# Route, scan and routed experts on one core: order of the work between tiles in two of the stages

## The reference

```python
scores = sigmoid(x @ router_w)
scores_grouped = (scores + router_bias).reshape(T, G, E // G)
group_scores = top_k(scores_grouped, 2).sum(-1)       # the best 4 groups stay open
top_k_index = top_k(masked, K)
tkw = scores[top_k_index] / sum * 2.5
gate, up = ragged_dot(xs, w_gate), ragged_dot(xs, w_up)   # rows sorted by expert, 512 columns
down = ragged_dot(silu(gate) * up, w_down)
shared = silu(x @ sw_gate) * (x @ sw_up) @ sw_down
```

## Time and profile before

| | |
|---|---|
| Median of three runs | 11768.19 us |
| Profiled execution | 11704.35 us |
| Its span | 11702.8 us |
| Mean granted TensorE clock | 0.985 |
| TensorE (PE) busy | 11303.2 us (97%) |
| Weight loads (PEld) | 9279.1 us (79%) |
| VectorE busy | 4611.8 us (39%) |
| ScalarE busy | 2989.1 us (26%) |
| GpSimd busy | 4299.9 us (37%) |

### The profile page before, as it was taken

The page is one execution under the profiler, slowest core; times in us unless marked ns, Lnnn a source line. Parts: engine busy times, 40 slices in busy tenths (PEclk is TensorE's granted clock), DMA queues, the critical chain, the costliest instruction groups (busy, mean ns, idle before and its releaser), DMA issues.

```text
span 11702.8 us, 200733 instructions
## 1 busy us (share of the span) xinstructions
PE 11303.2 (97%) x50496; PEld 9279.1 (79%) x50497; DVE 4611.8 (39%) x6239; ACT 2989.1 (26%) x4098; POOL 4299.9 (37%) x4236
## 2 busy tenths in 40 slices
PE   8999689998999999999999999999998999999998
PEld 7888467776888888888888888878887787888887
DVE  5666566664232323333323233232334323223222
ACT  2122244442222222222222222222223223222221
POOL 2555442222333333333333333333333333333333
PEclk9999799999999999999999999999999999999999
DMA  4333366675444444454544454454555545444443
GB/s 160 132 132 133 110 168 178 179 177 148 96 115 100 117 96 118 119 136 99 137 97 119 97 156 98 97 134 96 137 143 158 140 97 155 97 97 117 97 97 85
DMA packets 918208, 1451.51 MB, mean 124 GB/s; under 512 B 314530, under 2 KB 585058, under 8 KB 895048
## 3 DMA queue, kind: packets, MB, share of 16 engines
q0 software_dynamic: 212800, 623.06, 25.2%
q10 hardware_dynamic: 384512, 383.85, 11.8%
q1 hardware_dynamic: 320776, 443.28, 11.5%
HBM read 853.67 MB, written 596.15 MB: 124 GB/s over the span
## 4 chain that ended last, share of the span: by engine, by line
PE 64%; DVE 3%; issue 3%; DMA 3%; ACT 1%; DVEq 1%; ACTq 1%; POOL 0%; SPq 0%; POOLq 0%
PE pd L2002 22%; PE pg L66 7%; PE pg L67 7%; PE pu L66 7%; PE pg L68 7%; PE pu L68 7%; PE pu L67 7%; DMA activated<-av 2%; DVE w_lo L1908 2%; ACT w_hi L1817 1%; DMA aq<-activated 1%; ACTq L1589 1%; DVEq L1589 0%; DVE aT L1931 0%; DVE xT L1920 0%
## 5 line engine op out<-in xcount | busy, mean ns | idle before, releaser
L1772 POOL DMA_INDIRECT xq<-xn_rows,idx_q x2124 | 2191.5, 1032 | 936.6 <-issue 485.2
L1780 POOL DMA_INDIRECT out_rows<-y,idx_s x528 | 865.9, 1640 | 4472.0 <-issue 4462.2
L1956 DVE SCALAR_TENSOR_TENSOR av<-pu,scale,sg 128x512 f32<-128x512 f32 x528 | 396.6, 751 | 3598.3 <-PE pu L68 3537.3
L66 PE MATMUL pg<-w_hi,x_hi 128*128 128x512 f32 x4224 | 1645.5, 390 | 49.5 <-DVE x_lo L1924 39.4
L66 PE MATMUL pu<-w_hi,x_hi 128*128 128x512 f32 x4224 | 1644.2, 389 | 6.0 <-DVEq L1973 6.0
L67 PE MATMUL pg<-w_lo,x_hi 128*128 128x512 f32 x4224 | 1644.5, 389 | 0.0
L68 PE MATMUL pg<-w_hi,x_lo 128*128 128x512 f32 x4224 | 1644.4, 389 | 0.0
L67 PE MATMUL pu<-w_lo,x_hi 128*128 128x512 f32 x4224 | 1643.2, 389 | 0.0
L68 PE MATMUL pu<-w_hi,x_lo 128*128 128x512 f32 x4224 | 1643.2, 389 | 0.0
L1821 ACT ACTIVATE x_hi<-xT 128x1024 fp32r<-128x1024 f32 x530 | 562.8, 1062 | 3885.4 <-DVE xT L1920 3885.4
L2002 PE MATMUL pd<-w_hi,a_hi 128*128 128x512 f32 x4224 | 1143.6, 393 | 91.7 <-ACT a_hi L1837 91.3
(11 more groups left out here) (286 smaller groups left out, 14560.9 us busy)
## 6 DMA issues: line engine op xcount, KB each, us to landing
stage<-in_w_all SPq DMA_DIRECT2D x174, 1024.0 KB, 8.6
activated<-av ACTq DMA_DIRECT2D x528, 256.0 KB
aq<-activated ACTq DMA_DIRECT2D x528, 256.0 KB
rep<-steps ACTq DMA_DIRECT2D x192, 512.0 KB
xq<-xn_rows,idx_q POOLq DMA_INDIRECT x2124
xt<-in_x SPq DMA_DIRECT2D x64, 512.0 KB, 4.6
xn_rows<-xn SPq DMA_DIRECT2D x64, 512.0 KB, 2.6
xn_turned<-sx_hi SPq DMA_DIRECT2D x64, 512.0 KB
```

The lines of the kernel that those rows point to most:

```text
L66: m(dst, hi, whi[:, cols], start=begin, stop=False)
L1772: g.indirect_dma_start(out=xq[q][:, n], out_offset=None, in_=xn_q, in_offset=bass.IndirectOffsetOnAxis(ap=idx_q[q][:, n:n + 1], axis=0))\
L1780: g.indirect_dma_start(out=out, out_offset=bass.IndirectOffsetOnAxis(ap=idx_s[q][:, 0:1], axis=0), in_=y[q][:], in_offset=None, compute_op ...
L1956: v.scalar_tensor_tensor(out=av[:], in0=pu[:], scalar=scale[q][:].bitcast(F32), in1=sg[:], op0=ALU.mult, op1=ALU.mult).then_inc(av_ready, 1)
```

## The change

In the expert stage, three things change. VectorE turns the activations of t-1 ahead of the low parts of the down weights. The rows of t+1 (not t+2) are turned in tile t, and this stands on both engines near the head of the tile: behind `a_lo` on VectorE, behind `a_hi` on ScalarE, and so ahead of the silu and of the gate and up weights of the next expert. The reads of `fresh` and `runs` stand ahead of the waits and are made in every tile; gathers and lists of rows run two tiles ahead instead of three. In the route stage the choice of experts has five parts: old part 1 is cut behind its second search, parts 0 and 1 stand in k = 1, the one-hot part 2 in k = 2, part 3 in k = 3 and part 4 (old 3) in k = 0; turning `z` moves from k = 1 to k = 2 on TensorE, and its eviction from k = 2 to k = 3 on ScalarE.

```diff
@@ route stage, TensorE / ScalarE
-                    if k == 1 and not known(c, 0):
+                    if k == 2 and not known(c, 0):
                         z_turned(c - 1)
-                    if k == 2 and not known(c, 0):
+                    if k == 3 and not known(c, 0):
                         z_row(c - 1, 1 - r)
@@ route stage, VectorE
-                        route(c - 2, r, 3)
-                    if k < 3 and not known(c, 0):
-                        route(c - 1, 1 - r, k)
+                        route(c - 2, r, 4)
+                    if k and not known(c, 0):
+                        for part in ((0, 1), (2,), (3,))[k - 1]:
+                            route(c - 1, 1 - r, part)
@@ expert stage, SyncE / GpSimd
-                sp.wait_ge(quads_made, t + 2)
-                load_quads(t + 3, 1 - q)
+                sp.wait_ge(quads_made, t + 1)
+                load_quads(t + 2, q)
-                gather(t + 3, 1 - q, half + 1 + q)
+                gather(t + 2, q, half + 1)
@@ expert stage, ScalarE, tile(t, q)
+                x_high(t + 1, 1 - q)
+                new = value_of(act, fresh, t + 1, 1)
+                run = value_of(act, runs, t + 1, E)
                 act.wait_ge(gate_done, t + 1)
...
                 store_activated(t)
-                x_high(t + 2, q)
@@ expert stage, VectorE, begin(t)
-                    with dve.If(value_of(dve, fresh, t - 1, 1) > 0):
-                        lows(t - 1, (4, 5))
+                    new = value_of(dve, fresh, t - 1, 1)
+                    run = value_of(dve, runs, t - 1, E)
+                    turn_activated(t - 1)
+                    with dve.If(new > 0):
+                        lows(run, (4, 5))
                     with dve.Else():
                         dve.sem_inc(dve_passed, 1)
                 dve.sem_inc(down_weights, 1)
-                turn_activated(t - 1)
                 a_low(t - 1)
@@ expert stage, VectorE, tile(t, q)
-                with dve.If(value_of(dve, fresh, t + 1, 1) > 0):
-                    lows(t + 1, (0, 1))
+                turn_rows(t + 1, 1 - q, half + q)
+                x_low(t + 1, 1 - q)
+                new = value_of(dve, fresh, t + 1, 1)
+                run = value_of(dve, runs, t + 1, E)
+                with dve.If(new > 0):
+                    lows(run, (0, 1))
...
-                turn_rows(t + 2, q, half + 1)
-                x_low(t + 2, q)
```

More of the change, by code:

```diff
@@ L311, in chunk @@
                         store_xn(*later(c, k, 2))
-                    if k == 3 and not known(c, 0):
-                        store_z(c - 1, 1 - r)
                     if not ends(c, k, 1):
@@ L683, in route @@
             def route(c, i, part):
-                s = Steps(dve, rt_step, c * RT + (0, 7, 17, 21)[part], dve_passed)
+                s = Steps(dve, rt_step, c * RT + (0, 7, 14, 17, 21)[part], dve_passed)
                 if part == 0:
@@ L731, in route @@
                     s(last)
+                    assert s.n == 7, s.n
+                if part == 2:
                     s(v.tensor_copy(i8f[:], i8[:]))
@@ L741, in route @@
                     s(last)
-                    assert s.n == 10, s.n
-                if part == 2:
+                    assert s.n == 3, s.n
+                if part == 3:
                     s(v.tensor_reduce(w8[:].rearrange("p j k -> p (j k)"), prod[:], AX.X, ALU.add))
@@ L753, in route @@
                     assert s.n == 4, s.n
-                if part == 3:
+                if part == 4:
                     dve.wait_ge(rank_ready, c + 1)
@@ L795, in _ @@
             a_low(NT - 1)
-            route(NC - 2, 0, 3)
+            route(NC - 2, 0, 4)
             route(NC - 1, 1, 0)
             summed(NC - 1, J - 1)
-            route(NC - 1, 1, 1)
-            route(NC - 1, 1, 2)
-            route(NC - 1, 1, 3)
+            for part in range(1, 5):
+                route(NC - 1, 1, part)
 def scan_stage(nc, T, B, io):
@@ L1794, in _ @@
                 gather(q, q, 0, False)
-            gather(2, 0, 1)
             for q in range(2):
@@ L1844, in evict, with down_high @@
                 a.activation(y[q][:, h * 512:(h + 1) * 512], pd[h][:], ACT.Copy).then_inc(y_ready, 1)
-            def down_high(t):
-                run = 0 if isinstance(t, int) else value_of(act, runs, t, E)
+            def down_high(t, run):
                 wait_past(act, down_done, t * 2)
@@ L1855, in begin @@
                 if isinstance(t, int):
-                    down_high(t - 1)
+                    down_high(t - 1, 0)
                 else:
-                    with act.If(value_of(act, fresh, t - 1, 1) > 0):
-                        down_high(t - 1)
+                    new = value_of(act, fresh, t - 1, 1)
+                    run = value_of(act, runs, t - 1, E)
+                    with act.If(new > 0):
+                        down_high(t - 1, run)
                     with act.Else():
@@ L1870, in tile @@
                 a.activation(sg[:], pg[:], ACT.Silu).then_inc(sg_ready, 1)
-                with act.If(value_of(act, fresh, t + 1, 1) > 0):
-                    run = value_of(act, runs, t + 1, E)
+                with act.If(new > 0):
                     for k in (0, 1):
@@ L1909, in low, with lows @@
                     .then_inc(split_lo[q // 2], 1)
-            def lows(t, qs, known=None):
-                run = value_of(dve, runs, t, E) if known is None else known
+            def lows(run, qs):
                 for k in qs:
@@ L1968, in tile @@
                 activated(t, q, half)
-                with dve.If(value_of(dve, fresh, t + 1, 1) > 0):
-                    lows(t + 1, (2, 3))
+                with dve.If(new > 0):
+                    lows(run, (2, 3))
                 with dve.Else():
```

13 lines of the change are left out of this document (5 added, 8 removed).

## The result

| | before | after |
|---|---|---|
| Median, timed in turn on one chip | 11769.16 us (12 runs, 11751.63 to 11779.46) | 11749.31 us (12 runs, 11745.79 to 11756.90) |
| Ratio | | 0.9984, 95% interval 0.9976 to 0.9991 |
| Profiled execution, its span | 11704.35, 11702.8 us | 11747.12, 11745.5 us |
| Granted TensorE clock | 0.985 | 0.983 |

The changed kernel is 20 us faster by the timed runs. The two profiled executions say the opposite: the one of before was 47 us faster than any of its timed runs.

A forecast was written before the change was run, and what follows sets the result against it. TensorE was taken as busy in 8663.33 of the expert stage's 8843.00 us, so only its waits could pay. Route stage -19, clusters -28, lone switches +5 sum to -42: 11768 to 11726 us, range 11675 to 11792.

The forecast's parts named there:

- Route stage, -19: Waits for VectorE's `ssg` all go, 30 us; `bases` meeting another piece gives back 0.8 us in 14 chunks, 11 us.
- the piece of 9.1 us: Route stage, VectorE's old part 3 and part 0 at the end of k = 0; TensorE just does not wait behind it.
- A piece of 10.35 us: Route stage, head of k = 2: VectorE's 7.95 us plus 2.4 from `bases`, above the 9.1 us limit; a 0.8 us wait.
- The rule on the shared port: VectorE with two SBUF inputs and GpSimd reading SBUF contend, the later issued is blocked; the 2.4 us of `bases` move.
- Lone switches, +8: Expert stage, 17 lone expert switches: 2 us lost, 1.5 us of waits ahead of down gone, net +0.5 each.
- A is 5.2: Expert stage, tile ahead of a switch: A, the start of `aT` behind the gate's start, is 5.2 us.
- Clusters, -28: Expert stage, five groups of short experts with 11 switches: earlier `aT` and `a_hi` shorten the waits, 28 us together.
- The cluster of 25.0: Expert stage, five tiles at short experts taking 106.62 us, 25.0 over undisturbed tiles; forecast to gain about 7.
- loads alone bound the clusters, -65: Far end for the groups of short experts: gain 65 us if only loads and 6 `w_lo` a tile bound them.
- rival 1: The switches eat it: route stage -19, short-expert groups -10, lone switches +20, in all -9 us, 11759; chance 0.22.
- Rival 3: Slower: rows ahead of the silu wait for a late gather, delaying weights at all 28 switches; +45 us, 11813; chance 0.10.
- Starting from the median: Timed median 64 us above the profiled execution, not the program's difference; -42 applied to 11768 gives 11726 us.

The follow-up runs named there:

- the rows in front: Before, with only the rows of t+1 turned behind `a_lo` and `a_hi` and gathered two tiles ahead; 11743.92 us, ratio 1.0032, +37 us.
- the route part: Before with only the change's route-stage hunks, run twice: 11748.23 us, ratio 0.9971, and 11758.29 us, ratio 0.9976.
- the activations first: Before with one edit: VectorE turns the activations of t-1 ahead of `w_lo` 4 and 5; 11748.04 us, ratio 0.9965, -38 us.
- the rows back: Before with the change's expert-stage hunks, but rows turned two tiles ahead at the tile's end and gathered three ahead; 11667.06 us, ratio 0.9965.
- after again: The changed kernel, unaltered, timed again in turn with before; 11707.29 us, ratio 0.9999.
- The expert part: Before with only the change's expert-stage hunks; 11783.93 us, ratio 0.9998, -2 us.
- before again: The kernel before, without any edit, timed against itself; 11786.60 us, ratio 1.0000.
- the cut alone: Before with old part 1 of the choice of experts cut, part 0 and `z` staying where they were; 11748.02 us, ratio 0.9967.

## Why the time lay in the range and its terms did not hold

-20 us lies in the stated range, at about half of the forecast -42, and that is luck in good part: on chip B the same change measured 0, and the 23 us that the sum had from the expert stage came neither there nor on chip A. The mechanisms that it named are there; their sizes are not, and one of them (the rows in front) reaches further than the sum followed it.

**Route stage, -19: wrong in size on either kind of chip.** On chip B it is -1 to -4 us by the tiles (1251.4 and 1251.6 without the route part, 1250.1 and 1247.3 with it), on A and C -28 to -37. Two steps failed. First, the sum counted as gone the 30 us of all waits, with 0.8 us a chunk given back. In before, 11 of them stood in k = 1 (7.2 us) and went. (They stood behind the piece of 9.1 us, behind which the prediction said that TensorE just does not wait: it waited 0.65 us there, in 11 chunks.) The 12 in k = 2 (15.7 us, one of them behind the window of the earlier trace rows) did not: the piece at the end of k = 1 came out at 10.8 us (VectorE and GpSimd in after):

```profile
570.23 0.98 DVE L689 SCALAR_TENSOR_TENSOR zpre<-neg_s,mv,lg 128x96 f32<-128x96 f32 x4
...
573.07 3.02 DVE L701 TENSOR_TENSOR top<-mx 128x32 f32<-128x32 f32 x1
...
576.55 0.19 DVE L705 TENSOR_TENSOR gs<-top,m 128x32 f32<-128x32 f32 x1
...
581.05 0.69 DVE L667 TENSOR_TENSOR sa_lo<-stx,sa_hi 128x512 fp32r<-128x512 f32 x1
```

```profile
573.62 2.40 POOL L387 TENSOR_TENSOR bases<-xt,xn 128x1024 f32<-128x1024 f32 x1
```

`bases` met the piece where the prediction said; `top` took 3.02 us, `gs` of the same shape 0.19. A piece of 10.35 us was forecast, and the rows say 10.82. What was mis-sized is what such a piece costs: 0.8 us by the prediction, 1.6 us in each of 13 chunks by the wait, where old part 1 with its 11.0 us had cost 1.3. A piece that stays about as long as the old one keeps about the old cost. Why it is a little more than the old one's was not looked into. Second, the recorded execution did not have the stall of 2.8 us that the same code has on chip A; there the cut and the changed places of the parts gain more.

**The rule on the shared port.** The 2.4 us moved with the cut and did not vanish: `top` lasted until `bases` ended, at 576.09 and 576.02. That the two engines block each other is as the Trainium skill has it (SBUF — State Buffer, "Who interferes with whom"). Its other half, that the one issued first keeps the pair, these rows do not bear out: `top` is recorded 0.55 us ahead of `bases` and is the one that was held up, as the first `prod` is 0.11 us ahead of it in the earlier trace rows. The profile's starts on GpSimd are rough, so this does not settle it.

**Lone switches, +8 by the count and taken as +5: the mechanism right, three switches misjudged.** At the 14 lone ones it is 24.6 before and 24.1 after (chip A: 31.2 and 30.1): new waits ahead of gate, the old ones ahead of down gone, w - A at 5.3. Each side is near its forecast: the activations first gain 1.2 to 1.8 us a switch (1.5 forecast), the rows in front cost 1.2 to 1.7 (2 forecast). The three behind an expert of four tiles were counted among them at +0.5 each. They cost +5.6 each, 17 in all. The step that failed is "A is 5.2". There it is 9.9 at tile 144 (5.7 before), and these rows show where it comes from. VectorE, SyncE and ScalarE in before, at tiles 142 and 143 (gates at 5217.92 and 5235.15); ScalarE's row is the second eviction, which stands behind the load of `aq`, and its idle time is the wait for the store of `av`:

```profile
5230.96 0.75 DVE L1956 SCALAR_TENSOR_TENSOR av<-pu,scale,sg 128x512 f32<-128x512 f32 x1 [0.79 <-issue]
```

```profile
5237.10 2.09 SPq L1700 DMA_DIRECT2D stage<-in_w_all  x4
```

```profile
5254.66 0.60 ACT L1844 ACTIVATE y<-pd 128x512 f32<-128x512 f32 x1 [4.04 <-DMA activated<-av]
```

The same in after (gates at 5251.52 and 5267.94):

```profile
5268.20 0.75 DVE L1958 SCALAR_TENSOR_TENSOR av<-pu,scale,sg 128x512 f32<-128x512 f32 x1 [0.85 <-issue]
```

```profile
5269.96 0.61 SPq L1714 DMA_DIRECT2D scale<-slot_table  x1
5274.78 1.84 SPq L1702 DMA_DIRECT2D stage<-in_w_all  x4
```

```profile
5292.17 0.60 ACT L1843 ACTIVATE y<-pd 128x512 f32<-128x512 f32 x1 [9.62 <-DMA activated<-av]
```

Behind the first switch `av` comes 16.7 us behind its gate instead of 13.0, because the rows stand ahead of it on VectorE. SyncE's load of the scale waits for that `av`, and 4.8 us behind it in SyncE's order stand the next expert's weights: 6.8 us behind the gate of tile 143 instead of 1.95. The activations of tile 143 then come back later as well (`aq` issued 23.8 us behind the gate instead of 19.1), so A is 10 at the switch. Only 1.1 us of these 4.7 are a later `av` (12.5 behind the gate, 11.4 before); the other 3.6 are its store, which now takes 10.5 us to the issue of `aq` instead of 6.9, beside weight loads that were issued 4.9 us later. I had followed a switch for three tiles, and the lateness lasts longer than that. A turn from `aT` to `aT` has 12.1 us at the least against 16.32 a tile, where it had 8.9; with the rows back it has 10.1, and the three switches cost 6.2 us.

**Clusters, -28: half of it.** 109.1 in the recorded execution to 94.6 in after again, 113.1 to 98.8 on chip A, -14 in both; the first comparison's own trace of after has 102.3. The activations alone give -16 (113.1 to 96.8), rows back -18.5, so the rows in front cost only 2 to 4 us here. The step that failed is the gain that the earlier `aT` was given: with it alone 10 us of the 28 did not come, and which wait took them was not traced. The cluster of 25.0, forecast to gain 7, got 2.2 longer. In it stands the one wait of after's rows for a gather in the middle of the stage; before has none:

```profile
8882.51 1.25 DVE L1919 STREAM_TRANSPOSE xT<-xq 128x1024 f32<-128x1024 f32 x1 [3.51 <-DMA xq<-xn_rows,idx_q]
```

The three other traces with activations first and rows in front have it at the same tile, 2.4 to 3.0 us. No run came near the other end of the range (loads alone bound the clusters, -65): the lowest has 90.6 us.

**Sum.** Chip B: -4 for the route stage, 0 + 17 - 14.5 = +2 for the switches, together -2 and measured 0. Chip A: -37 and 0 for the parts. The first comparison had -20, between the two, and after's route stage had stalls there (ahead of `spg`, 6.2 us in 10 pieces) and 1280.8 us. So -20 is most likely the route part in the presence of stalls. That is not shown for this comparison itself, since none of the timed runs of before in it left a trace. The expert part, forecast at -23, gave nothing on chip A. The forecast of -42 was closest in kind to rival 1 (the switches eat it). What rival 1 had against it was true too: the wait ahead of down was real and worth 38 us by itself. Rival 3 named the right edit and, but for the one wait above, the wrong cause: the +37 comes with the place of the rows. The shorter lead of the gathers was part of that run and was not tried by itself, but its trace has no `xT` waiting for a gather behind the start of the stage.

**Starting from the median.** The prediction called the 64 us between the recorded execution and the timed ones a difference of the execution and not of the program. The program is the same, but most of what differs between chips A and B, 55 of 78 us, lies in the very stage that the change cuts, and the recorded execution looks like chip B's (route tiles 1252.1 against 1251.4 and 1251.6). So a term read from that trace need not be the term where the kernel was timed.

**What was to show it.** As forecast: an undisturbed tile of 16.32 us, `a_hi` at 18.1 (under 40), 27 waits ahead of gate (about 28), the lone switch at 50.35 (50 to 51.5), the `ssg` waits all in k = 2. Not as forecast: waits ahead of up for `w_lo` hardly came, the cluster's window is 64.33 (59 to 63), `ssg` has 20.3 us (8), and the gate waits are up to 11.7 us long (1 to 5). By the prediction's own words it is wrong if the waits for `ssg` stay or if `xT` waits for gathers in the middle of the stage. The first moved and stayed in sum; the second happened once.

## What to carry to other kernels

- Time each move of a combined change alone. Here one moved line was worth -38 us and its companion +37, and the whole showed neither.
- Where work is put at the head of a tile, follow the round (result, store, load, next tile) until it is back at rest, and look whether the next disturbance comes before that, also through a queue that waits for the result and holds the next loads.
- When the recorded execution stands outside the timed runs, look in a second trace for where they differ before a term is taken from the first.

## What the runs showed of the hardware

- Three chips ran the same program in 11707.4, 11785.6 and 11785.9 us, at granted clocks of 0.982 to 0.985. Between chips A and B, 55 us of the 78 lie in the route stage's tiles (1307 against 1252) and 18 ahead of the scan stage, in idle times at the same instructions in most chunks. What stalls VectorE there is open: the profile names it "remote" or "issue", nothing more. So is whether it goes with the chip.
- The stall ahead of `i8f` (10 of them, 27.7 us, in before again) is not there with the route part (chips A and C) or with the cut (chip C). Others stand elsewhere instead: with the cut alone VectorE's `bases` waits 21.3 us in 5 pieces for "remote", and TensorE has 20 pauses of over 0.3 and up to 1.0 us ahead of `spg` in k = 0 (9 of up to 0.5 in before again). On chip B there is no such pause.
- A VectorE instruction of 0.2 us next to GpSimd's 2.40 us `bases` took 3.02 us.
- A store of 256 KB and the issue of the load behind it were 6.9 us apart at tile 143 of before and 10.5 in after, where the weight loads beside it were issued later; in 38 undisturbed tiles of before (15 to 32 and 180 to 199) they are 2.3 apart in the median.
